# W_base multiplied before and during attention, the attention output multiplied by its column sums

## The reference, cut to what matters

```python
x = x + xattn(layernorm(x), ctx)     # softmax(q ctx^T) ctx, 49 blocks of 512 keys
x = x + attn(layernorm(x), Wq, bq, Wk, bk, Wv, bv)
x = x + ffn(layernorm(x), W_base, b_base, W_gate, A, B)
# attn: q, k, v of [64 d] x [32 or 8 heads]; k and v repeated 4 times over heads
#   per token: scores[d, e] = sum_h q[d, h] k[e, h] / 8; softmax over e; out[d, h] = sum_e p[d, e] v[e, h]
# ffn: y = x W_base^T + b_base; 8 experts by W_gate, the best 2 weighted, rank 16: y += (x A^T * route) B
```

## Time and profile before

| | |
|---|---|
| median of 3 runs | 2553.24 us (2550.48 to 2562.08) |
| profiled execution | 2560.45 us, its span 2558.6 us |
| PE, DVE, ACT, POOL busy | 96%, 77%, 42%, 49% of the span |
| DMA | 476 MB, mean 186 GB/s |

### The profile page before, as it was taken

One profiled execution on the slowest core, in us unless ns is written; L12 is line 12 of the kernel. 1 busy time (PEld: TensorE's weight loads), 2 busy tenths in 40 slices (PEclk: granted clock), 3 DMA queues, 4 the chain that ended last, 5 costly groups with the idle time before them and its releaser, 6 DMA issues.

```text
span 2558.6 us, 35034 instructions
## 1 busy us (share of the span) xinstructions
PE 2458.9 (96%) x11342; PEld 2025.2 (79%) x11342; DVE 1975.5 (77%) x2668; ACT 1081.6 (42%) x1547; POOL 1265.1 (49%) x896
## 2 busy tenths in 40 slices
PE   6999999999999999999999999999999999894799
PEld 4888888888888888888888888888888888763677
DVE  7788888888888888888888887787878778532668
ACT  4444444444444444444444444444444444222323
POOL 4455556565556556655665565555555555410000
PEclk9999999999999999999999999999999999996579
DMA  9787887788788778878887877787777777667046
GB/s 243 200 217 182 215 202 195 200 209 212 194 206 213 195 196 209 206 197 213 201 204 194 210 190 189 191 196 184 192 184 186 188 188 192 166 138 113 5 85 145
DMA packets 377515, 476.14 MB, mean 186 GB/s; under 512 B 48707, under 2 KB 265795, under 8 KB 374853
## 3 DMA queue, kind: packets, MB, share of 16 engines
q1 hardware_dynamic: 373894, 454.68, 73.3%
q0 software_dynamic: 3584, 20.97, 2.6%
HBM read 467.74 MB, written 7.86 MB: 186 GB/s over the span
## 4 chain that ended last, share of the span: by engine, by line
PE 89%; DMA 4%; DVE 3%; SPq 2%; ACT 1%; POOL 1%; issue 1%; DVEq 0%; ACTq 0%
PE ps L1004 28%; PE ps L1006 28%; PE ps L1005 28%; PE ps L1013 2%; DMA raw<-in_L_attn_Wv_dram 1%; DMA q_t<-qk_dram 1%; DVE ch_lo L768 1%; PE ps L1034 1%; SPq L330 1%; DMA raw<-in_ctx_dram 1%; POOL nat_lo L475 1%; PE ps L1197 1%; DVE tr L764 1%; ACT nat_hi L557 1%; PE ps L1165 0%
## 5 line engine op out<-in xcount | busy, mean ns | idle before, releaser
L475 POOL TENSOR_TENSOR nat_lo<-raw,nat_hi 128x512 fp32r<-128x512 f32 x800 | 1172.8, 1496 | 933.3 <-ACT nat_hi L557 931.0
L768 DVE TENSOR_TENSOR ch_lo<-tr,ch_hi 128x512 fp32r<-128x512 f32 x848 | 949.9, 1120 | 362.6 <-ACT ch_hi L534 360.7
L534 ACT CAST ch_hi<-tr 128x512 fp32r<-128x512 f32 x848 | 517.2, 621 | 876.2 <-PE ps L1006 857.1
L1004 PE MATMUL ps<-ch_hi,xt_hi 128*128 128x512 f32 x1696 | 674.5, 398 | 8.1 <-DVE ch_lo L768 7.7
L1006 PE MATMUL ps<-ch_hi,xt_lo 128*128 128x512 f32 x1696 | 663.5, 391 | 0.0
L1005 PE MATMUL ps<-ch_lo,xt_hi 128*128 128x512 f32 x1696 | 662.9, 391 | 0.0
L1004 PE MATMUL ps<-nat_hi,pt_hi 128*128 128x512 f32 x1568 | 610.3, 389 | 2.9 <-DVE pt_lo L698 2.9
L1006 PE MATMUL ps<-nat_hi,pt_lo 128*128 128x512 f32 x1568 | 610.2, 389 | 0.0
L1005 PE MATMUL ps<-nat_lo,pt_hi 128*128 128x512 f32 x1568 | 610.0, 389 | 0.0
L764 DVE STREAM_TRANSPOSE tr<-quart 128x512 f32<-128x512 f32 x848 | 592.8, 699 | 3.9 <-DMA quart<-in_L_ffn_W_base_dram 3.8
L557 ACT CAST nat_hi<-raw 128x2048 fp32r<-128x2048 f32 x208 | 397.5, 1911 | 276.9 <-PE ps L1006 215.3
(11 more groups left out here) (126 smaller groups left out, 941.7 us busy)
## 6 DMA issues: line engine op xcount, KB each, us to landing
quart<-in_ctx_dram SPq DMA_DIRECT2D x392, 512.0 KB, 8.3
raw<-in_ctx_dram SPq DMA_DIRECT2D x196, 1024.0 KB, 7.8
wq_in<-in_L_attn_Wq_dram POOLq DMA_DIRECT2D x16, 1024.0 KB, 11.9
quart<-in_L_ffn_W_base_dram SPq DMA_DIRECT2D x32, 512.0 KB, 8.6
wq_dram<-wq_out POOLq DMA_DIRECT2D x16, 256.0 KB, 2.3
raw<-in_L_attn_Wk_dram SPq DMA_DIRECT2D x4, 1024.0 KB, 6.3
raw<-wq_dram SPq DMA_DIRECT2D x4, 1024.0 KB, 5.2
raw<-in_L_attn_Wv_dram SPq DMA_DIRECT2D x4, 1024.0 KB, 17.6
```

Source lines behind the costliest of these rows:

```text
L475: last = pool.tensor_tensor(nat_lo[:, j, t], raw[:, j % 2, t], nat_hi[:, j, t].bitcast(F32), ALU.subtract)
L534: act.copy(ch_hi[:, c % RING_CH, :], tr[:, c % RING_TR, :]).then_inc(chunk_hi, 1)
L768: dve.tensor_tensor(ch_lo[:, c % RING_CH, :], tr[:, c % RING_TR, :], ch_hi[:, c % RING_CH, :].bitcast(F32), ALU.subtract).then_inc(chunk_s ...
L1004: pe.matmul(out_, a_hi, b_hi, start=start, stop=False)
```

## The change

- **In the loop**: Wq is summed two chunks per pair of blocks in the first 8 pairs. In each of the last 16 pairs 128 rows of W_base are loaded (`win`, 1 MB), turned by DVE in four transposes and stored by SP to `wt_dram` in four stores of 256 KB; POOL then adds the columns in fours (3 instructions), DVE turns the result and SP stores it to `wp_dram`. Nothing of W_base is turned after the loop.
- **K, Q and V**: weights go through four buffers of their own (`w_rows`), and the loads of Q and V stand ahead of the stores and reads of q and k. x1 and its statistics are made piece by piece, and the transposes of the first token tile stand before the last weighted piece.
- **x1hat times W_base** (64 chunks) is multiplied: 16 chunks after V, among the transposes of A, gate and V and the wait for `q_t`; 48 in attention, three to a step. Chunks are now loaded by POOL, one DMA of 256 KB each, straight into `tr`; POOL makes `ch_lo` for one chunk in four, DVE for the others.
- **The router and A** multiply x1hat after the last steps of attention and the centred o by column sums of A and gate.
- **After attention** 16 chunks of sums of W_base meet the centred o (four of every quarter of columns), POOL making `ch_lo` of every second one, and POOL adds b_base to x2. The transposed third norm is gone.

The diff, cut to its core. First the work on W_base in the loop, `sum_win` on POOL (in the second block of a pair) and `turn_win` on DVE:

```diff
+            win4 = win[:].rearrange("p r (n j) -> p (r n) j", j=REP)
+            def sum_win(m):
+                pool.wait_ge(win_turned, m * 5 + 4)
+                pool.tensor_tensor(win4[:, :, 0], win4[:, :, 0], win4[:, :, 1], ALU.add).then_inc(win_half, 1)
...
+                pool.tensor_tensor(stage[:], win4[:, :, 0], win4[:, :, 2], ALU.add).then_inc(win_summed, 1)
+            def turn_win(m, k):
...
+                elif k < 4:
+                    dve.wait_ge(wt_stored, m * 80 + 16 * k)
...
+                dve.transpose(dst[:].rearrange("p (c r j) -> p c r j", c=4, j=SQ), src).then_inc(win_turned, 1)
+TURN_AFTER = {(0, 8): 0, (0, 12): 1, (0, 16): 2, (1, 4): 3, (1, 14): 4}
```

POOL's loads of the chunks (`by_pool(w)` holds for every fourth chunk up to 63 and for every second one from 64 on; `lo_base` waits for ACT's `chunk_hi`, and that for the load):

```diff
+            def load_base(w):
...
+                elif by_pool(w - RING_TR):
+                    pool.wait_ge(pool_split, pool_splits(w - RING_TR))
+                else:
+                    pool.wait_ge(chunk_split, dve_splits(w - RING_TR))
+                pool.dma_start(tr[:, w % RING_TR, :], of).then_inc(base_loaded[w % RING_TR], 16)
...
+            for w in range(RING_TR, BASE_W):
+                load_base(w)
+                if by_pool(w):
+                    lo_base(w)
```

PE in attention:

```diff
             for o in range(OCT + 2):
+                w = PRE_W + STEP_W * o
                 if 2 <= o < OCT:
                     pe.wait_ge(att_shifted, o - 1)
                     pair_scores(o)
+                if o < OCT:
+                    base_chunk(w)
                 if 1 <= o <= OCT:
                     pe.wait_ge(att_exped, o)
-                    plain_group(H_ATT + o - 1, [att_e[:, (o - 1) % 2, a * P:(a + 1) * P] for a in range(4)])
+                    plain_group(h_att(o - 1), [att_e[:, (o - 1) % 2, a * P:(a + 1) * P] for a in range(4)])
+                if o < OCT:
+                    base_chunk(w + 1)
                 if o >= 2:
+                    rows_out(o - 2)
+                if o < OCT:
+                    base_chunk(w + 2)
+                if o == OCT:
+                    router_chunks(0, 6)
+            router_chunks(6, 12)
```

PE at the end; ACT, which now copies the transposed `hw`, does it behind its last rounding of a chunk:

```diff
+            sum_chunks(0)
+            sum_chunks(1)
+            pe.wait_ge(router_kept, TT)
+            sum_chunks(2)
+            pe.wait_ge(hw_ready, TT)
...
+            pe.wait_ge(hwt_ready, 1)
+            experts_out(0)
+            sum_chunks(3)
+            for ob in range(1, FB):
+                experts_out(ob)
```

More of the change, by code:

```diff
@@ L310, in perceiver_block, with in_pairs, in_w_pairs @@
         LATE_AFTER = {1: 6, 3: 7}
-        def in_pairs(eng, work, start=1, end=PAIRS):
-            with eng.Fori(start, end) as i:
+        def in_pairs(eng, work):
+            with eng.Fori(1, WQ_PAIRS) as i:
                 for step in range(2):
                     work(Turn(i, step))
+        def in_w_pairs(eng, work):
+            with eng.Fori(0, PAIRS - WQ_PAIRS) as m:
+                for step in range(2):
+                    work(Turn(m, step, WQ_PAIRS), m)
         block = stack.enter_context(nc.Block())
@@ L493, in _ @@
[L493 to L496, removed]
-            for turn in REST:
[L498 to L501, removed]
+                    pool.dma_start(wq_in[:], wq[bass.ds(i * (2 * P) + step * P, P)].rearrange("p d h -> p (d h)")
+                                   ).then_inc(wq_loaded, 16)
@@ new lines, in w_pair @@
+            def w_pair(turn, m):
+                if turn.step == 1:
+                    sum_win(m)
+                split_block(turn)
+            in_w_pairs(pool, w_pair)
+            for turn in REST:
+                w_pair(turn, LAST_M)
+            for j in range(PIECES - 1):
+                pool.wait_ge(nat_hi_ready, NB * PIECES + j + 1)
+                for t in range(KT):
+                    last = pool.tensor_tensor(nat_lo[:, j, t], w_rows[j][:, t], nat_hi[:, j, t].bitcast(F32), ALU.subtract)
+                last.then_inc(nat_ready[j], 1)
@@ L844, in iteration @@
                         add_pieces(turn, (ADD_AFTER[c],))
+                    if m is not None and (turn.step, c) in TURN_AFTER:
+                        turn_win(m, TURN_AFTER[turn.step, c])
             iteration(FIRST)
@@ new lines, in router_chunks @@
+            def router_chunks(first, end_):
+                for c in range(first, end_):
+                    for t in range(TT):
+                        if c == 0:
+                            pe.wait_ge(base_kept[t], FB)
+                        last = product(t, x_part(xt_hi, c, t), x_part(xt_lo, c, t), ag_hi[:, c, :], ag_lo[:, c, :],
+                                       start=(c == 0), stop=(c == DC - 1))
+                    if c == DC - 1:
+                        last.then_inc(router_done, 1)
```

940 lines of the change are left out of this document (638 added, 302 removed).

## The result

Slower: the median is 2589.81 us (2589.35 to 2600.70, 4 runs) against 2552.93 (4 runs) of the kernel before, timed beside it. The ratio is 1.0143 (95% interval 1.0116 to 1.017); the forecast was 2513, with a range to 2550. The profiled execution took 2590.12 us, its span 2588.5, so it stands within 0.4 us of the median.

The account below looks back on a forecast made before the run. PE bounds the loop, so work added to other engines there is free; after it PE is starved in stages. Start of K plus five stages, 2226 + 73 + 35 + 99 + 25 + 60 = 2518 us span, median 2513; range 2480 to 2550.

Parts of the forecast that it names:

- (c): Attention: 50.5 to 99 us, 16 steps of 6.2 us with three chunks each, PE near POOL's limit; bounds 88 and 115.
- POOL's cycle: After V, four chunks' issues, landing, ACT's rounding and POOL's subtraction in a row: 7.2 us, or 5.4 per attention step.
- The landing: Time for a 256 KB chunk load by POOL to arrive after V: taken as 3.0 us, between 2.3 and 5.2.
- The rival "the loads land in 2 us": After the loop, POOL isn't the limit, as loads land in 2 us or are always ahead: 2474 us, chance 0.13.
- (b): From V's end to the first attention step: 22.4 to 35 us; bounds 29 and 45.
- The loop: Loop of block pairs: the added DVE, POOL and DMA work fits in their slack, costing 0; bound 32 us.
- The rival that names the mechanism: The loop stalls: DVE waits for `wt_stored` with `ch_lo` behind, PE runs dry; 32 us, 2545 us, chance 0.09.
- K, Q and V: Stage of the K, Q and V projections after the loop: 107 to 73 us; bounds 70 and 80.
- (d): From attention to the sums of W_base: 47 to 25 us, expected between 20 and 30.
- (e): The end, 16 chunks of sums of W_base with POOL cycles of 6.1 us: 103.5 to 60 us; bounds 35 and 70.
- The half-clock rival: Clock stays at half in attention, steps of 10.6 us, +70 us: 2583 us, slower; chance 0.09.
- The rule on POOL's issues: POOL's DMA issues wait for DVE on the shared port; as a rival 32 us, 2545 us, chance 0.04.

Follow-up runs that it names:

- run 1: Changed kernel with POOL issuing loads up to three chunks ahead of its rounding wait, the first three before V's end: 2534.2 us, ratio 0.9912.
- run 2: Changed kernel with all subtractions (`ch_lo`) on DVE, POOL only issuing loads: 2536.73 us, ratio 0.9907.
- run 10: Changed kernel with POOL issuing one load ahead of its rounding wait, instead of none: 2566.8 us, ratio 1.0035.
- Run 5: Changed kernel with one of the six part reads of k and q left, scores over 8 of 48 rows: 2581.35 us, ratio 1.0088.
- run 3: Changed kernel with the experts' B read in rows of 1 KB instead of 64 bytes: 2597.13 us, ratio 1.0143.
- run 6: run 1 with some reads of q and k widened to 16 rows of `q_t` in place of 8: 2533.5 us, ratio 0.9908.
- run 4: Changed kernel without loading, turning, summing and storing W_base in the loop; chunks read from W_base as it lies: 2588.24 us, ratio 1.0113.
- run 9: Changed kernel with DVE's second and third transposes of a W_base window one chunk later: 2585.31 us, ratio 1.0111.

## Why the prediction was wrong, point by point

**The step that failed is (c), and with it the way POOL's cycle was used.** The forecast saw the cycle and its cause: POOL waits on its own chunk with the next loads queued behind. It costed it at 7.2 us, divided by four and multiplied by three (5.4 a step), set this beside 6.2 of PE's, and took the larger. These two are not independent. The loads are released by a chunk that PE must then use, and the small matmuls wait for passes that stand behind the same chunk in the programs of DVE and ACT. The measured cycle is 10.25 us, 7.7 for three chunks. With the loads ahead the step is 6.47, so the estimate of PE's own step was right to 4%, and 15 x (8.06 - 6.47) = 24 of the 28 us missed in (c) are this coupling; the others are 15 x (6.47 - 6.2). A wrong price of the landing isn't the reason: where nothing else stood in the cycle, it took 7.45 us. Runs 1, 2 and 10 form a series: ratio 1.0143 with no load ahead, 1.0035 with one, 0.9912 with three, 0.9907 with POOL out of the way.

**The landing** was taken as 3.0 us and has a median of 4.2 and a maximum of 15.8. The rival "the loads land in 2 us" fell. In run 1, where the landings are covered, the median is 3.2 us and one still took 17.4, so the time came back without the landings having to be short. The Trainium skill (DMA: Bandwidth & Descriptors, "Anatomy of one DMA — SWDGE (gpsimd) path") gives a fit of 2.0 us plus the bytes over 436e3 a us, by which I estimate 2.6 us for 256 KB; here the fastest of the 64 took 3.0, so for loads among other traffic the rows decide.

**(b)** The allowance for reads beside the loads, 3 us a cycle, was the term mis-sized. One load there took 15.74 us on the chain of the changed kernel, where 3.0 and 3 more were allowed, and POOL stood for it:

```profile
2328.07 1.27 POOL L646 TENSOR_TENSOR ch_lo<-tr,ch_hi 128x512 fp32r<-128x512 f32 x1 [6.42 <-ACT ch_hi L837]
2329.30 2.16 POOL L641 DMA_DIRECT2D tr<-wt_dram  x4
2347.52 1.39 POOL L646 TENSOR_TENSOR ch_lo<-tr,ch_hi 128x512 fp32r<-128x512 f32 x1 [16.06 <-ACT ch_hi L837]
```

Run 5 shows that the reads of k and q, with the store of q that waits behind them, are 12 us of this stage, about the 13.7 missed; the size of B's pieces is no part of it (run 3), nor the width of the reads (run 6). That the loads are issued only behind V's end costs some 10 us as well (the four runs with early loads against the others). The two overlap and aren't to be added. The stage varies: 38.4 us in run 1, 52.9 in run 10.

**The loop** was taken as 0. The rival that names the mechanism (DVE waits for a store, `ch_lo` behind it) had 0.09, with 32 us; it is real, at 11.2 of the 13.1 us. The forecast compared a landing near 8 us with about 9 of cover and 11 between transposes, and took that for enough; the median landing is 7.6, but in 11 of the transposes between 830 and 1800 us the store came up to 1.7 us too late, and in the first pair with this work 5.38 us:

```profile
815.25 0.71 DVE L1098 STREAM_TRANSPOSE stage<-win 128x512 f32<-128x512 f32 x1 [5.38 <-DMA wt_dram<-stage]
```

One chunk more of distance took away nearly all of it: over the whole loop DVE waits 30.6 us for these stores in the changed kernel and 2.2 in run 9. By bytes the forecast was right about the DMA share: 0.86, not over the 0.90 allowed for. The other 1.9 us of the 13.1 were not tried; with no work on W_base at all (run 4) the loop ends at 2191.81 us, no sooner than the 2191.43 of run 9, so they don't lie there.

**K, Q and V**, with the last weighted pieces, came out near the forecast, 4.2 us over, with PE busy 98.5 of 102.5 us: the four row buffers did what was said of them.

**(d)** was 8.4 us over, and the half clock is the reason. PE is busy 30.66 of the 33.4 us, the clock is 0.50 for all of it, and 120 matmuls of 136 columns follow each other there, 0.21 us apart. In run 1 PE comes out of attention at a clock of 1.00, and the same matmuls stand 0.11 us apart. Its (d) and (e), split at the first sum of W_base:

```profile
2458.60:2477.86 19.26, 18.13 (x176) 17.16 (x175) 6.99 (x15) 7.02 (x17) 2.36 (x3) 1.00 0.13 43
2477.86:2529.80 51.94, 34.09 (x116) 22.00 (x115) 40.55 (x65) 9.67 (x21) 22.37 (x18) 0.87 0.25 81
```

At full clock (d) is 19.3 us, under the 25 of the forecast. In the changed kernel PE waited 2.12 and 2.98 us between its last chunk of attention and the router, in run 1 0.34; the late chunks cost (d) 14 us in this way.

**(e)** was right, 63.1 for 60, by a cycle costed step by step where PE is not near the limit and nothing else goes round with it. Five cycles with the additions between them took 37.1 us (2530.68 to 2567.76), where 38.6 were costed, and PE then waited 8.64 us for the copy of `hw`, as was said. The sum itself has a slip: 42 or 43.4, 5.5 and 4.2 make 52 to 53 and not 54. The cycle is costly here too: in run 1 (e) is 51.9 us, 11 shorter.

**The half-clock rival** fell. The clock in attention is 0.92, and with PE fed 1.00. Half clock for a whole stage came only in (d), behind PE's waits. That the rival's 2583 lies near the measured time is a coincidence: its 70 us were to come from a slow attention, and the measured 70.5 come from all six rows of the table.

**The rule on POOL's issues** did not come true. All 80 loads were issued in 0.54 to 0.56 us each. The 3.1 us of the Trainium skill cited in the forecast (SBUF — State Buffer, "SBUF: two separate sides") are for an issue beside a VectorE `tensor_copy`; DVE's passes beside the issues here in attention are nearly all `TENSOR_TENSOR` and `TENSOR_REDUCE` (none a copy from SBUF to SBUF), so these runs don't test that figure.

**The change as such** was worth its work: with the loads ahead of the wait it is 0.9% faster than the kernel before (interval 0.6 to 1.1%), and with the later transposes and the wider reads 1.3%. The 2513 of the forecast would have been a ratio of 0.984; even the best version stays at 0.9871.

## What to carry to other kernels

When an engine both issues loads and waits for the result of one of them, put every load whose place is free ahead of the wait; here that one reordering was worth 2.3% of the time of a whole kernel, and all of it lies in stages that are a tenth of that time (272 us). When two cycles share a ring, don't take the larger of the two periods: follow one item all the way round, through the program of every engine it passes, and count what stands behind it there. And where a wait is to be hidden by distance in the program, measure that distance against the slowest landings, not against the median one.

## What the runs showed of the hardware that was not expected

A 256 KB load issued by POOL lands in 3.0 us at best and 4.2 in the middle, but in every run with all the reads of q and k one load of (b) took 13.3 to 27.2 us, though the DMA share of that stage is only 0.80 in the changed kernel. Cutting those reads to a sixth brought the longest to 9.6; reading them twice as wide left it at 19.1. What exactly holds such a load back is open. One load issued ahead leaves the time spread over 24 us (2554.52 to 2578.64, 12 runs), three loads ahead over 10 (2531.16 to 2541.4, but 4 runs only), which fits with these landings being exposed or covered, but was not tried by itself.
